# Attention: weighing in twelve half pieces, and turned tiles and projections one at a time

## The chip, the core and the metric

The kernel runs on one core of a Trainium2 chip. The metric is the device time of one execution in microseconds (us). TensorE (PE in the profile) multiplies and transposes into PSUM; ScalarE (ACT), VectorE (DVE) and GpSimd (POOL) work beside it, each through its own list of instructions in order, and they are tied together by semaphores. TensorE's clock is granted at one of two levels, 2.4 or 1.2 GHz; the profile gives it as 1.00 and 0.50.

## What is computed

Four layers on x of shape (4, 1024, 128): causal attention with 16 heads of 8 columns, a mixture of 8 experts, a sigmoid message layer, and the mixture again. The change touches the attention alone:

```python
k = _layernorm((x @ Wk).reshape(b, t, h, s), kln_w, kln_b)
q = _layernorm((x @ Wq).reshape(b, t, h, s), qln_w, qln_b)
v = (x @ Wv).reshape(b, t, h, s)
dot = jnp.einsum('bqhs,bkhs->bhqk', q, k) * scale
dot = jnp.where(causal, dot, -jnp.inf)
attn = jax.nn.softmax(dot, axis=-1)
out = jnp.einsum('bhqk,bkhs->bqhs', attn, v).reshape(b, t, e)
return out @ Wo + bo
```

## The kernel before

The attention works through 16 **groups**: 4 batches of 1024 tokens, and in each 4 groups of 4 heads. A head's queries and keys lie in 32 rows (the values in high and low parts, and the shift by the row's maximum), so that the four heads of a group fill the 128 rows of TensorE, and each product of queries and keys uses 32 rows of it and all 128 columns.

A group has 40 **steps**. In step i TensorE makes score product i of the group (`scores`, line 640; up to 512 columns) into one of six PSUM banks, and about one product for the maxima of the *next* group (`maxima_unit`, line 627). ScalarE takes the score bank away with an exponential (`weights`, line 822); VectorE takes the other away with a maximum (lines 1150 and 1155). The banks go round in a ring: unit n waits until unit n - 6 is taken.

Beside these products TensorE has **blocks** of another form. **Weighing** (`weigh`, line 660) multiplies the exponentials of key tile j by the values: 128 rows and 32 columns for each of the four heads, side by side, into the accumulator `o_acc` of two banks. The trace shows each of these float32 products as two records: `x16` there is 8 products. Tile j weighs for all queries at or after it: piece j has 1024 - 128 j columns, so pieces 0 to 3 run over both halves of the tokens. **Turns** (line 594) transpose four 128x128 tiles with all of TensorE: keys and queries of the group after next, the shifted queries (`turn_low`, `turn_high`), the results `oT`, and in the first group of a batch the tokens. **Projections** (line 612) are made for the next batch in groups with g == 1.

The function `sequence` writes the order of a group out by hand, and every engine reads the same order. Before the change it places the blocks so, by the step after which they come:

- weighing: pieces 0, 1, 2, 3, 4, 5 after steps 15, 20, 27, 32, 36, 39; pieces 6 and 7 of the group before together after step 5 (`WEIGHED_AFTER`, `WEIGHED_LATE`);
- `empty_out` at step 9: ScalarE copies all of `o_acc` to `oT`; both halves of `oT` are turned together after step 17, and VectorE divides them (`normalise`);
- keys and queries for later at 31, 32, 34 and 35; `turn_high` at 3, `turn_low` at 21;
- projections in pairs at 21, 23, 26 and 29, in groups with g == 1 only.

I call steps 0 to 14 of a group its **first stretch** and steps 15 to 39 its **second stretch**; they are told apart in the trace by the start of the exponentials.

## Time and profile before

| | us |
|---|---|
| median of three runs | 2903.04 |
| lowest and highest | 2891.97, 2903.37 |
| the profiled execution | 2907.53 |
| its span, first to last instruction | 2905.7 |
| attention: first to last exponential of its 16 groups | 65.9 to about 754 |
| PE, DVE, ACT busy in the whole span | 2671.1, 1784.2, 1597.3 |

The profile is of one execution. The rows below are of four groups of the attention, from 200.6 to 364.9 us: the fourth group of the first batch (200.6 to 237.2), the first of the second batch (to 275.0), the second (to 323.4) and the third (to 364.9). Their lengths are 36.6, 37.8, 48.4 and 41.5 us, and this pattern returns in the other batches. "Busy" counts overlapping products once, so it says nothing of how many run side by side. In the view in order of time, the first number is the start; the time that a block takes from its neighbours is best read from its start to the start of what comes after it.

### The profile page before, as it was taken

How to read it: one execution, taken by the hardware profiler on the slowest of the kernel's cores; microseconds unless marked ns; L12 is line 12 of the kernel's file. 1: busy time of each engine (PE TensorE's matmuls, PEld its weight loads, DVE VectorE, ACT ScalarE, POOL GpSimd, SP SyncE). 2: the span in 40 equal slices, each digit the busy share in tenths (PEclk: the TensorE clock that was granted, in tenths of full speed). 3: DMA queues.
4: the chain of work that ended last, by engine and by line, in shares of the span. 5: the costliest groups of instructions: out<-in, count | busy, mean ns of one | idle time of the engine just before them, and what ended most of it. 6: DMA issues, size and time to landing. Idle time of an engine off the chain costs nothing. (4 is left out here: it accounts for less than half of the span.)

```text
span 2905.7 us, 54730 instructions
## 1 busy us (share of the span) xinstructions
PE 2671.1 (92%) x18814; PEld 1641.2 (56%) x18814; DVE 1784.2 (61%) x4087; ACT 1597.3 (55%) x2918; POOL 811.9 (28%) x1179
## 2 busy tenths in 40 slices
PE   6988998999678979999999999999999999996897
PEld 4444443444367855666556555555555555554786
DVE  7677677667364755555665556555556655556556
ACT  2566666666554445555555556565566555554343
POOL 3142423423425321111111121112121133322542
PEclk7688877767899989999999999999999999997998
DMA  9000000000323438888888888877888788884222
GB/s 162 3 1 1 1 1 1 1 1 15 119 78 110 136 80 196 197 196 196 199 192 198 192 196 190 192 183 183 186 190 192 184 200 193 199 193 175 61 82 85
DMA packets 187362, 374.82 MB, mean 129 GB/s; under 512 B 44257, under 2 KB 99690, under 8 KB 185738
## 3 DMA queue, kind: packets, MB, share of 16 engines
q1 hardware_dynamic: 178506, 354.15, 51.1%
q0 software_dynamic: 8640, 17.84, 1.7%
q8 instruction: 129, 2.11, 0.3%
q14 instruction: 87, 0.71, 0.1%
HBM read 38.10 MB, written 39.86 MB: 27 GB/s over the span
## 5 line engine op out<-in xcount | busy, mean ns | idle before, releaser
L2996 DVE STREAM_TRANSPOSE m_turned<-m_sig 128x1024 f32<-128x1024 f32 x512 | 613.7, 1228 | 423.1 <-ACT m_sig L2766 222.6
L2589 PE MATMUL m_v_ps<-m_sig,m_tok 128*64 128x512 f32 x2048 | 468.1, 599 | 0.0
L2602 PE MATMUL m_v_ps<-m_sigT,m_tok 128*64 128x256 f32 x4064 | 461.2, 380 | 0.6 <-DMA m_sigT<-m_turned 0.6
L822 ACT ACTIVATE a_prob<-a_bank 128x512 f32<-128x512 f32 (+1 forms) x640 | 321.7, 564 | 222.0 <-PE a_bank L640 199.7
L2573 PE MATMUL m_f_ps<-m_swap,m_own 64*128 64x512 f32 x1536 | 426.0, 404 | 16.6 <-DMA m_swap<-m_own 8.4
L2573 PE MATMUL m_f_ps<-m_own,m_swap 64*128 64x512 f32 x1536 | 426.1, 404 | 0.0
L2602 PEld LDWEIGHTS m_v_ps<-m_sigT,m_tok 128*64 128x64 f32 x4064 | 289.9, 137 | 196.0 <-issue 59.2
L2766 ACT ACTIVATE m_sig<-m_f_ps 128x1024 f32<-128x1024 f32 x256 | 248.4, 1023 | 251.0 <-issue 152.6
L2862 POOL TENSOR_TENSOR m_own<-m_uv,m_own 128x1024 fp32r<-128x1024 f32 x64 | 151.9, 2373 | 810.5 <-ACT m_own L2728 810.5
L2573 PEld LDWEIGHTS m_f_ps<-m_swap,m_own 64*128 64x128 f32 x1536 | 271.7, 186 | 99.5 <-ACT m_sig L2752 25.9
L627 PE MATMUL a_bank<-a_kT,a_qT 32*128 32x512 f32 (+3 forms) x768 | 277.6, 496 | 31.8 <-DVE a_maxima L1155 20.2
L2752 ACT ACTIVATE m_sig<-m_f_ps 128x512 f32<-128x512 f32 x512 | 264.5, 604 | 38.7 <-PE m_f_ps L2573 37.0
L2589 PEld LDWEIGHTS m_v_ps<-m_sig,m_tok 128*64 128x64 f32 x2048 | 135.7, 136 | 265.2 <-issue 264.8
L2573 PEld LDWEIGHTS m_f_ps<-m_own,m_swap 64*128 64x128 f32 x1536 | 271.4, 186 | 5.6
L640 PE MATMUL a_bank<-a_qmT,a_kT 32*128 32x512 f32 (+3 forms) x768 | 247.0, 501 | 25.9 <-DVE a_maxima L1155 13.2
L1150 DVE TENSOR_REDUCE a_first_max<-a_bank 128x1 f32<-128x512 f32 x256 | 165.1, 684 | 91.8 <-PE a_bank L627 89.4
L640 PEld LDWEIGHTS a_bank<-a_qmT,a_kT 32*128 32x128 f32 x768 | 112.4, 220 | 167.5 <-issue 110.5
L2778 ACT CAST m_v1T_hi<-m_v_ps 128x256 fp32r<-128x256 f32 x128 | 47.8, 373 | 285.4 <-PE m_v_ps L2602 271.6
L660 PE MATMUL a_o_acc<-a_prob,v 128*32 128x512 f32 (+3 forms) x1536 | 198.1, 639 | 5.9 <-POOL a_prob L968 3.6
L627 PEld LDWEIGHTS a_bank<-a_kT,a_qT 32*128 32x128 f32 x768 | 138.1, 226 | 108.4 <-DVE a_maxima L1155 50.2
L3005 DVE TENSOR_TENSOR m_v1T_lo<-m_v_ps,m_v1T_hi 128x256 fp32r<-128x256 f32 x128 | 54.2, 423 | 217.0 <-ACT m_v1T_hi L2778 205.6
L1773 PE MATMUL f_y_ps<-f_w_down,f_innerT 128*128 x1136 | 153.3, 278 | 25.8 <-DVE f_raw L2183 17.9
(505 smaller groups left out, 4426.5 us busy)
## 6 DMA issues: line engine op xcount, KB each, us to landing
m_sigT<-m_turned SPq DMA_DIRECT2D x2042, 128.0 KB, 2.3
m_swap<-m_own SPq DMA_DIRECT2D x64, 256.0 KB
f_t_rows<-f_sent_rows SPq DMA_DIRECT2D x142, 65.0 KB
f_sent_rows<-a_proj SPq DMA_DIRECT2D x34, 260.0 KB, 8.9
m_swap<-m_own SPq DMA_DIRECT2D x64, 128.0 KB
f_h<-back_rows SPq DMA_DIRECT2D x8, 512.0 KB, 5.0
rows<-back_rows SPq DMA_DIRECT2D x6, 512.0 KB, 4.2
x<-in_L_attn_a_x_dram SPq DMA_DIRECT2D x4, 512.0 KB, 4.8
```

Source lines behind the costliest of these rows:

```text
L627: mm = pe.matmul(out[:, col:col + k1 - k0], qT[G % 2][rows, qt * P:(qt + 1) * P], kT[G % KEPT_KEYS][rows, k0:k1], start=True, stop=True)
L640: mm = pe.matmul(out[:, col:col + q1 - q0], kT[G % KEPT_KEYS][rows, j * P:(j + 1) * P], qmT[G % 2][rows, q0:q1], start=True, stop=True)
L660: mm = pe.matmul(o_acc[h * STACK:(h + 1) * STACK, q0:q1], v1[:, j, g * GROUP + h, :], weights_at[:, h, q0 - off:q1 - off], start=(j == 0), ...
L822: act.activation(to[:, h, start:start + width], src[:, 0:width], ACT.Exp).then_inc(u.free(), 1)
L1150: ins = dve.tensor_reduce(first, scores, AX.X, ALU.max)
L1773: mm = pe.matmul(y_ps[:, 0:DIM], innerT[p][:, ib * P:(ib + 1) * P], w_down[:, ds(e * INTER + ib * DIM, DIM)], start=(ib == 0), stop=(ib == ...
L2573: mm = pe.matmul(f_ps[s][:, cols], tile_of(u[rows, :], j + s * SIDE), v[rows, cols], start=start, stop=stop)
L2589: mm = pe.matmul(v2_ps[h * RANK:(h + 1) * RANK, :], tok[p][:, 0, j + s * SIDE, :], sig[j % 2][s][:, h * HALF:(h + 1) * HALF], start=(j == ...
L2602: mm = pe.matmul(v1_ps[h * RANK:(h + 1) * RANK, g * 2 * P:(g + 1) * 2 * P], tok[p][:, 1, jj, :], sigT[g][:, :, 2 * h:2 * h + 2, jj, :].rea ...
L2752: ins = act.activation(sig[1][s][:, cols], f_ps[s][:, cols], ACT.Sigmoid)
L2766: act.activation(sig[j % 2][s][:, :], f_ps[s][:, :], ACT.Sigmoid).then_inc(sig_ready, 1)
L2996: dve.transpose(turned[g][:, :, q, :, :], sig[j % 2][s][:, :].rearrange("p (t j a) -> p j t a", j=4, a=STACK)).then_inc(turn_ready, 1)
```

## The change

Each piece of weighing for tiles 0 to 3 is cut into a part for the low half of the queries (columns 0 to 511) and one for the high half, so that there are twelve pieces (tile, half) of at most 512 columns. They are placed anew. `o_acc` is emptied in two halves with a semaphore each. The turns of `oT`, keys, queries and tokens, and each projection, get a step of their own. Number and size of the products stay as they are. `late_made` and `state` only hand the numbers of the score units over from group to group.

```diff
-        WEIGHED_AFTER = {15: (0,), 20: (1,), 27: (2,), 32: (3,), 36: (4,), 39: (5,)}
-        WEIGHED_LATE = (6, 7)
+        WEIGHED_AFTER = {9: (0, 0), 12: (1, 0), 14: (0, 1), 18: (1, 1), 24: (2, 0), 26: (3, 0), 28: (2, 1), 31: (3, 1), 36: (4, 1)}
+        WEIGHED_LATE = {1: (5, 1), 4: (6, 1), 5: (7, 1)}
...
+        PROJECTED_AT = (17, 19, 21, 23, 25, 27, 30, 32)
...
-                if prev and i == 3:
+                if prev and i == 2:
                     yield "turn_high", 0
-                if prev and i == 5:
-                    for n in WEIGHED_LATE:
-                        yield "weigh", n
-                if prev and i == 9:
+                if prev and i in WEIGHED_LATE:
+                    yield "weigh", WEIGHED_LATE[i]
+                if prev and i == 7:
+                    yield "empty_out", 1
+                if i == 29:
                     yield "empty_out", 0
-                if two_ahead and i in (31, 32, 34, 35):
-                    yield ("keys", "queries")[i // 34], (31, 32, 34, 35).index(i) % HALVES_OF
+                if two_ahead and i in (16, 30, 34, 38):
+                    yield ("keys", "queries")[i in (30, 38)], (16, 30, 34, 38).index(i) // 2
...
-                if prev and i == 17:
-                    for n in range(HALVES_OF):
-                        yield "turn_out", n
-                if prev and g == 0 and i in (23, 29):
-                    for n in range(HALVES_OF):
-                        yield ("turn_tokens", "project_out")[i == 29], n
+                if prev and i == 11:
+                    yield "turn_out", 1
+                if i == 33:
+                    yield "turn_out", 0
+                if prev and g == 0 and i in (17, 19, 23, 25):
+                    yield ("turn_tokens", "project_out")[i // 23], (17, 19, 23, 25).index(i) % HALVES_OF
...
-                    if i in (21, 23, 26, 29):
-                        for n in range(2):
-                            yield "project", 2 * (21, 23, 26, 29).index(i) + n
+                    if i in PROJECTED_AT:
+                        yield "project", PROJECTED_AT.index(i)
...
+                q0, q1 = max(j * P, half * HALF), (half + 1) * HALF
+                weights_at, off = prob_of(j, q0)
+                last = j == (half + 1) * HALF_T - 1
+                for h in range(GROUP):
+                    mm = pe.matmul(o_acc[h * STACK:(h + 1) * STACK, q0:q1], v1[:, j, g * GROUP + h, :],
+                                   weights_at[:, h, q0 - off:q1 - off], start=(j == 0), stop=last)
+                if last:
+                    mm.then_inc(weighed[half], 1)
...
-                act.wait_ge(weighed, G + 1)
-                act.copy(oT[:, :], o_acc[:, :]).then_inc(o_free, 1)
+                act.wait_ge(weighed[half], G + 1)
+                act.copy(half_of(oT, half), half_of(o_acc, half)).then_inc(o_free[half], 1)
```

Two places of TensorE's list show it, both in the fourth group (qmT1 and kT0 are its shifted queries and keys; kT1 and qT0 belong to the next group, whose maxima are made; `a_o_acc` is a piece of weighing). The first is around steps 11 to 15, before:

```order
L640 MATMUL a_bank4<-a_qmT1,a_kT0 128x512
L627 MATMUL a_bank5<-a_kT1,a_qT0 128x512
L640 MATMUL a_bank0<-a_qmT1,a_kT0 128x512
L627 MATMUL a_bank1<-a_kT1,a_qT0 128x512
L640 MATMUL a_bank2<-a_qmT1,a_kT0 128x512
L627 MATMUL a_bank3<-a_kT1,a_qT0 128x512
L640 MATMUL a_bank4<-a_qmT1,a_kT0 128x512
L627 MATMUL a_bank5<-a_kT1,a_qT0 128x512
L660 MATMUL a_o_acc<-a_prob0,v1 32x512 x8
```

And now, steps 9 to 12:

```order
L628 MATMUL a_bank0<-a_kT1,a_qT0 128x512
L660 MATMUL a_o_acc<-a_prob0,v1 32x512 x4
L641 MATMUL a_bank1<-a_qmT1,a_kT0 128x512
L628 MATMUL a_bank2<-a_kT1,a_qT0 128x512
L641 MATMUL a_bank3<-a_qmT1,a_kT0 128x512
L628 MATMUL a_bank4<-a_kT1,a_qT0 128x512
L595 MATMUL a_bank5<-ident,a_oT 128x128 x4
L641 MATMUL a_bank0<-a_qmT1,a_kT0 128x512
L628 MATMUL a_bank1<-a_kT1,a_qT0 128x512
L660 MATMUL a_o_acc<-a_prob1,v1 32x384 x4
```

Piece 0, eight products in one go after ten steps of 32-row products alone, has become two pieces of four, and the first of them, a turn of `oT` and the low piece of tile 1 now stand within steps 9 to 12.

The second place is around steps 32 to 35 of the same group, before:

```order
L660 MATMUL a_o_acc<-a_prob0,v1 32x128 x4
L660 MATMUL a_o_acc<-a_prob1,v1 32x512 x4
L640 MATMUL a_bank4<-a_qmT1,a_kT0 128x384
L627 MATMUL a_bank5<-a_kT1,a_qT0 128x512
L640 MATMUL a_bank0<-a_qmT1,a_kT0 128x384
L594 MATMUL a_bank1<-ident,q_st 128x128 x4
L627 MATMUL a_bank2<-a_kT1,a_qT0 128x512
L640 MATMUL a_bank3<-a_qmT1,a_kT0 128x384
L594 MATMUL a_bank4<-ident,q_st 128x128 x4
L627 MATMUL a_bank5<-a_kT1,a_qT0 128x512
```

And now, from step 31 on:

```order
L660 MATMUL a_o_acc<-a_prob1,v1 32x512 x4
L641 MATMUL a_bank2<-a_qmT1,a_kT0 128x384
L628 MATMUL a_bank3<-a_kT1,a_qT0 128x512
L641 MATMUL a_bank4<-a_qmT1,a_kT0 128x384
L628 MATMUL a_bank5<-a_kT1,a_qT0 128x512
L595 MATMUL a_bank0<-ident,a_oT 128x128 x4
L641 MATMUL a_bank1<-a_qmT1,a_kT0 128x384
L595 MATMUL a_bank2<-ident,k_st 128x128 x4
L628 MATMUL a_bank3<-a_kT1,a_qT0 128x512
```

The low part of tile 3 has gone from in front of its high part to step 26, and a turn of the low half of `oT`, that of the group itself, has come in at step 33.

## Rows read from the trace of the kernel before

**Rows 1.** Busy time by stretch, two stretches to a group; PEclk is the granted clock.
```profile
core 0: us, PE busy (x) PEld busy (x) DVE busy (x) ACT busy (x) POOL busy (x), PEclk, DMA share, GB/s
200.60:210.70 10.10, 9.37 (x51) 4.65 (x48) 8.79 (x37) 8.76 (x18) 5.85 (x15) 0.65 0.01 2
210.70:237.20 26.50, 26.24 (x177) 11.89 (x176) 17.73 (x52) 14.49 (x30) 3.21 (x9) 0.87 0.00 1
237.20:247.30 10.10, 7.97 (x56) 3.64 (x58) 9.34 (x39) 9.43 (x18) 5.90 (x15) 0.87 0.01 2
247.30:275.00 27.70, 27.64 (x201) 14.17 (x199) 20.85 (x61) 15.66 (x33) 3.20 (x9) 0.92 0.00 1
275.00:293.50 18.50, 11.95 (x60) 5.82 (x64) 15.79 (x64) 12.77 (x22) 5.85 (x15) 0.60 0.01 2
293.50:323.40 29.90, 29.83 (x196) 14.09 (x189) 17.38 (x51) 19.13 (x49) 3.23 (x10) 0.96 0.00 1
323.40:339.00 15.60, 10.07 (x52) 4.85 (x48) 14.29 (x41) 11.74 (x21) 10.23 (x12) 0.60 0.01 2
339.00:364.90 25.90, 25.46 (x177) 11.90 (x176) 17.76 (x53) 14.55 (x31) 15.98 (x22) 0.91 0.00 1
```

**Rows 2.** Who waited for whom, 200.6 to 237.2: in total, times, longest.
```profile
ACT a_prob L822 <- PE a_bank L640: 12.8, 8, 3.6
```

**Rows 3.** TensorE in order of time, clock high: start, length, line, operation.
```profile
214.35 0.38 PE L640 MATMUL a_bank<-a_qmT,a_kT 32*128 32x256 f32 x1
...
215.01 1.09 PE L594 MATMUL a_bank<-ident,a_oT 128*128 128x128 f32 x8
...
217.87 1.71 PE L660 MATMUL a_o_acc<-a_prob,v 128*32 128x384 f32 x16
...
219.51 0.49 PE L640 MATMUL a_bank<-a_qmT,a_kT 32*128 32x512 f32 x1
...
220.16 0.66 PE L594 MATMUL a_bank<-ident,q_st 128*128 128x128 f32 x4
220.75 0.50 PE L640 MATMUL a_bank<-a_qmT,a_kT 32*128 32x512 f32 x2
...
234.25 1.06 PE L660 MATMUL a_o_acc<-a_prob,v 128*32 128x512 f32 x8
...
235.24 0.46 PE L640 MATMUL a_bank<-a_qmT,a_kT 32*128 32x256 f32 x6
...
235.90 0.85 PE L660 MATMUL a_o_acc<-a_prob,v 128*32 128x384 f32 x8
...
236.68 0.49 PE L640 MATMUL a_bank<-a_qmT,a_kT 32*128 32x512 f32 x1
```

**Rows 4.** The same view where the clock is at half.
```profile
525.03 1.12 PE L594 MATMUL a_bank<-ident,k_st 128*128 128x128 f32 x4
526.07 0.79 PE L627 MATMUL a_bank<-a_kT,a_qT 32*128 32x512 f32 x1
...
534.71 0.79 PE L627 MATMUL a_bank<-a_kT,a_qT 32*128 32x512 f32 x1
...
535.86 1.94 PE L660 MATMUL a_o_acc<-a_prob,v 128*32 128x512 f32 x8
537.72 0.59 PE L640 MATMUL a_bank<-a_qmT,a_kT 32*128 32x256 f32 x3
```

**Rows 5.** Busy time by stretch as in rows 1, cut where the clock changed.
```profile
327.30:339.40 12.10, 7.09 (x22) 3.21 (x21) 11.33 (x22) 8.74 (x14) 6.73 (x7) 0.50 0.01 2
339.40:343.00 3.60, 3.60 (x17) 0.60 (x16) 1.05 (x2) 0.17 (x1) 3.38 (x4) 0.50 0.00 0
343.70:360.60 16.90, 16.46 (x116) 8.53 (x115) 12.98 (x39) 10.99 (x23) 10.54 (x14) 1.00 0.00 1
521.30:541.00 19.70, 19.45 (x90) 8.12 (x83) 7.72 (x21) 8.21 (x16) 5.39 (x13) 0.50 0.00 1
613.40:655.40 42.00, 40.21 (x175) 20.88 (x177) 27.24 (x92) 23.78 (x47) 12.26 (x23) 0.50 0.00 1
```

More of the change, by code:

```diff
@@ L416, in attention_phase @@
         queries_rounded, queries_ready = sem("a_queries_rounded"), sem("a_queries_ready")
-        unit_full, kept, weighed, o_free = (sem(n) for n in ("a_unit_full", "a_kept", "a_weighed", "a_o_free"))
+        unit_full, kept, weighed, o_free = sem("a_unit_full"), sem("a_kept"), *([sem(f"a_{n}_{half}") for half in ("low", "high")] for n in ("weighed", "o_free"))
         unit_free = [sem(f"a_unit_free{i}") for i in range(RINGS)]
@@ L700, in count, with group @@
                 pe.matmul(out[:, 2 * ROUTE:2 * ROUTE + P], k["ones"][:, :], k["below"][:, :], start=True, stop=True).then_inc(unit_full, 1)
-            def group(u, b, g, prev, prep, follows, shifted, stacks, high=None):
+            def group(u, b, g, prev, prep, follows, shifted, stacks, late_made, normed, high=None):
                 G = GROUPS * b + g
-                ahead, last_of_prev = (g + 1) % GROUPS, u.n
-                score_made, next_stacks, z_made, normed, turned, shifted_high = {}, [], [], [], [], high
+                ahead, normed = (g + 1) % GROUPS, dict(normed)
+                score_made, next_stacks, z_made, turned, shifted_high = {}, [], [], [], high
                 for what, n in sequence(g, prev, prep, follows, stage_of(b, g)):
@@ L709, in group @@
                         scores(u, G, n, {0: (shifted,), FIRST_HIGH: (shifted_high,)}.get(n, ()))
-                        for piece in SCORES[n][0]:
-                            score_made[piece[0]] = u.n
+                        for j, q0, _ in SCORES[n][0]:
+                            score_made[j, q0 // HALF] = u.n
                     elif what == "keys":
@@ L746, in group, with before_batch @@
                         count(u)
-                return shifted, next_stacks
+                return shifted, next_stacks, {piece: score_made[piece] for piece in WEIGHED_LATE.values()}, {0: normed[0]}
+            def before_batch(shifted, stacks, late_made, normed):
+                return (shifted - UNITS_BATCH, [n - UNITS_BATCH for n in stacks], {piece: n - UNITS_BATCH for piece, n in late_made.items()},
+                        {0: normed[0] - UNITS_BATCH})
             u = Units(0, 0)
@@ L761, in _ @@
             high = turn_shifted(u, 0, 0, 1)
-            shifted, stacks = group(u, 0, 0, False, False, True, shifted, (), high)
+            state = group(u, 0, 0, False, False, True, shifted, (), {}, {}, high)
             for b in range(BATCH - 1):
@@ L771, in _ @@
             for g in (1, 2, 3):
-                shifted, stacks = group(u, b, g, True, False, g < GROUPS - 1, shifted, stacks)
-            for n in WEIGHED_LATE:
-                weigh(u, b, GROUPS - 1, n, u.n)
-            normed = [turn_out(u, GROUPS * BATCH - 1, n) for n in range(HALVES_OF)]
+                state = group(u, b, g, True, False, g < GROUPS - 1, *state)
+            _, _, late_made, normed = state
+            for piece in WEIGHED_LATE.values():
+                weigh(u, b, GROUPS - 1, *piece, late_made[piece])
+            normed[1] = turn_out(u, GROUPS * BATCH - 1, 1)
             turned = [turn_tokens(u, n, normed[n]) for n in range(HALVES_OF)]
@@ L858, in group @@
                     elif what == "empty_out":
[L859 to L860 removed]
+                        empty_out(G - n, n)
+                        if g == 0 and n and prev:
                             values(u, projects)
@@ L1428, in _ @@
                 made = group(u, link, b, g, True, False, g < GROUPS - 1, masked_by, made)
-            for n in range(HALVES_OF):
-                normalise(u, link, GROUPS - 1, n)
+            normalise(u, link, GROUPS - 1, 1)
             u.n += HALVES_OF
```

53 lines of the change are left out of this document (20 added, 33 removed).

## The prediction

> **What bounds the kernel now.** I read the busy time by stretch first. In the second stretch of each group TensorE is busy almost without a break: 26.24 of 26.5 us in the fourth group, 27.64 of 27.7, 29.83 of 29.9 and 25.46 of 25.9 in the three after it, while VectorE has 17.4 to 20.9 and ScalarE 14.5 to 19.1 [rows 1]. In the first stretch it is otherwise: VectorE has 8.79 of 10.1, 9.34 of 10.1, 15.79 of 18.5, 14.29 of 15.6, and TensorE has room, most of it in the last two (11.95 of 18.5, 10.07 of 15.6) [rows 1]. Then the waits: over the fourth group ScalarE's exponentials waited 12.8 us for score products [rows 2]. So TensorE sets the pace for steps 15 to 39, and VectorE (with ScalarE close by) for steps 0 to 14. No engine sets it for the whole group, and the time is more than the sum of any of them: 36.6 us, against 26.5 of VectorE and 23.3 of ScalarE.
>
> The third view is the granted clock. It is 0.60 to 0.87 in the first stretches and 0.87 to 0.96 in the second ones [rows 1]. Cut at its changes, it shows a cycle: it is at half (1.2 GHz) while TensorE has ten steps of 32-row products and waits (327.3 to 339.4, busy 7.09 of 12.1 us), still at half during piece 0, sixteen records in one go in which TensorE is busy all 3.60 us, and at full (2.4 GHz) after it [rows 5]. Where the drop in the first stretch costs little, since VectorE bounds it, piece 0 at half clock costs its doubling.
>
> **The change part by part.** Prices are from start to start, clock full [rows 3]: pieces 1 together (384 and 512 columns) 219.51 - 217.87 = 1.64 us; a lone 512-column piece 235.24 - 234.25 = 0.99; a lone 384-column piece 236.68 - 235.90 = 0.78; a turn of four tiles 220.75 - 220.16 = 0.59; one step of products alone between two blocks 220.16 - 219.51 = 0.65; two steps between two blocks 215.01 - 214.35 = 0.66. The last two say that products of different heads run side by side, so an interruption after every second step costs TensorE little and one after every step doubles the steps.
>
> *Cutting.* A piece cut in two costs 0.99 + 0.78 - 1.64 = 0.13 us more. The fourth group goes from 14 blocks to 20, so about 0.8 us are added per group.
>
> *Moving.* Out of the second stretch go pieces (0,0), (0,1), (1,0) and (5,1): 2 x 0.99 + 2 x 0.78 = 3.5 us, and half the turn of oT, 0.6. They come into the first stretch, where TensorE had to wait for VectorE.
>
> *TensorE's sum for a fourth group, all at full clock.* Six 512-column pieces 5.9; two of 384, 1.6; for two of 256 and two of 128 no row stands alone, and the slope between 512 and 384 (0.21) gives 0.57 and 0.36, together 1.9. Eight turns 4.7. The 40 steps lie in 20 runs, about 0.66 each, 13.2; four of these have three or four steps, and I add 0.5 for each. The sum is 29.3 us. VectorE's is 8.79 + 17.73 = 26.5, and where it set the pace it was busy 9.34 of 10.1 us, 92% [rows 1], so 28.8. The bounds are nearly equal and are joined by a ring of six banks, so neither is hidden fully: I take **31 us**, against 36.6, a gain of 5.6. If they overlapped perfectly it would be 29.3; if they hid nothing more than now, the group loses only the doubling of piece 0, (3.60 of rows 5 less 2 x 0.99) = 1.6, less 0.8 for cuts. Both ends stay for the range. I take 31 since moving 3.5 us changes the balance directly.
>
> *First group of a batch.* VectorE has 9.34 + 20.85 = 30.2, over 0.92 = 32.8; two turns of tokens and two projections of the output are added to TensorE's sum. I take 35 against 37.8: a gain of 3.
>
> *Second group.* Its first stretch, 18.5 us, is set by VectorE (the token moments) and stays. The second loses 3.5 + 0.6, but eight projections stand alone in place of four pairs: four more joints at 0.13 and some five runs cut from two steps to one. I take a gain of 1.5 in 48.4.
>
> *Third group.* The first stretch (15.6) is VectorE's. With the clock full the second would be about 20 in place of 25.9.
>
> *ScalarE and GpSimd.* The copy of oT was one instruction; two halves add a fraction of one microsecond per group to an engine with 23.3 busy of 36.6. The high half is asked for at step 7, two steps after piece (7,1) rather than four; TensorE runs up to three steps ahead in the ring, so I cost that wait at nothing; at worst it is one piece, 0.4. The masks of tiles 0 and 1 come after steps 3 and 7, and their pieces wait at 9 and 12: five or more steps, some 3 us. The tail of the last group changes by under 1 us.
>
> **The clock** is the term with two signs. For a high clock: the ten steps of 32-row products before piece 0 become four at most (6 to 9), and six steps in the second stretch become three. Against it: after the change nothing like piece 0 is left; the longest piece is eight records. The trace shows half clock that did not end although TensorE was busy 19.45 of 19.7 us (521.3 to 541.0) and 40.21 of 42.0 (613.4 to 655.4) [rows 5]; these hold all other pieces and turns, and what ended them was the next piece 0. At half clock a turn costs 526.07 - 525.03 = 1.04, a 512-column piece 537.72 - 535.86 = 1.86, two steps 535.86 - 534.71 = 1.15 [rows 4]. A whole group of the new order at half: pieces 6 x 1.86 + 2 x 1.45 + 3.2 = 17.3, turns 8.3, 20 runs x 1.1 = 22: 47.5 us against 36.6. VectorE's long steps in the second and third groups (token moments, sums of squares) will still let the clock drop there. The projections of a second group and of a first group's output lie densely, so I expect the clock to come back there; in a third group I give it one chance in two, and two in three that the fourth group runs at full.
>
> The Trainium skill ("TensorE: Matmul & The Clock Gate", section "Why this matters for your kernels") advises to keep TensorE continuously busy to have the full clock. By that rule the evener order would always be at full, which is the second rival below; the two half-clock stretches of rows 5, busy 95% and more, speak against it being enough.
>
> **The sum.** Per batch: second group -1.5; third 0 (-5.5 or +5, even); fourth 2/3 x -5.6 + 1/3 x +8 = -1; the next first group 7/8 x -3 + 1/8 x +8 = -1.6; together -4. Three batches, -12. The old order's own long half-clock stretches, 19.7 and 42.0 us [rows 5], are part of the time before: at prices near double on about half of the work they cost some 8 and 12 us, and the chances above already stand for their like after. That is -20. The opening group and the last three give -3. Together -35, from the profiled execution's 2907.5 to 2872.5; the median shown is 4.5 lower, and I predict **2870 us** (-1.1%).
>
> **The rivals.**
> - *Wash* (2889 to 2917, centre 2903): TensorE is no longer alone the bound, and VectorE's and ScalarE's turns in the ring take what it gives back; only piece 0's doubling goes, and the cuts eat it. For it: VectorE already at 85 to 92% in the first stretches. Against: ScalarE's 12.8 us of waiting for scores.
> - *Always full clock*: no drop in the third and fourth groups and the first. Per batch -5.5 - 5.6 - 3 - 3 = -17, three times, with the 20 above: -71, so 2832.
> - *Slower, by the clock*: once at half in a second or third group, nothing lifts it before the next projections. Third +5, fourth +11, first +7, second -1: +22 per batch, +66 in three, less the 20: +46, so 2949. It decides when more than about half of the fourth groups run at half.
>
> **How the numbers follow.** Forecast (2845 to 2888) 0.50, wash 0.20, always full 0.10, slower by the clock 0.20. A measurement of this kernel can tell about 0.5% (14.5 us) from no change. Faster by more than that: 0.50 + 0.10 = 0.60, within it 0.20, slower 0.20. The range takes forecast, always full and wash, and a little of the slow side: 2825 to 2920.
>
> **What would show it.** Forecast: fourth groups of 30 to 33 us; TensorE and VectorE both at 85% or more in each stretch; ScalarE's wait for scores in one group down from 12.8 to under 8; mean clock of the attention at least 0.80. The slow rival: granted clock 0.50 across whole third and fourth groups, groups over 44 us, TensorE busy throughout. The wash: groups of 35 to 37 at full clock with TensorE waiting for VectorE. I am wrong on the runs if two steps between blocks take 1.2 us in place of 0.66 at full clock. Outside the attention nothing should move by more than a microsecond or two.

## The result, and the profile after

| | before | changed |
|---|---|---|
| median of four runs | 2903.05 | 2992.2 |
| lowest and highest | 2891.97, 2903.37 | 2975.54, 3000.57 |
| the profiled execution | 2907.53 | 2999.59 |

The changed kernel takes 1.031 times as long, with a 95% interval of 1.0253 to 1.0366. I had forecast 2870 us and a range up to 2920: the forecast is wrong in sign, and the time lies outside the range. My slower rival had the right mechanism, but put it at 2949 us, 43 below the measured time.

From the page of the changed kernel: its span, the busy time of the engines, and the granted clock in 40 slices of the span (tenths of full speed).

```profile
span 2997.8 us, 54746 instructions
...
PE 2820.3 (94%) x18814; PEld 1686.7 (56%) x18814; DVE 1794.6 (60%) x4087; ACT 1618.3 (54%) x2934; POOL 810.6 (27%) x1179
...
PEclk6565555657568998999999999999999999998998
```

TensorE executes as many records as before (18814), but is busy for 2820.3 us in place of 2671.1. Over the attention (up to 890 us, the first 12 slices) the clock is mostly at 5 and 6 tenths. VectorE is up by 10.4 us and ScalarE by 21.0. The loss is one of speed, not of waiting.

Busy time by stretch in the changed kernel, with the columns of [rows 1]: the fourth group of the first batch, and the first, second and third of the second batch; then a long piece of them; then the whole attention and what follows it.

```profile
core 0: us, PE busy (x) PEld busy (x) DVE busy (x) ACT busy (x) POOL busy (x), PEclk, DMA share, GB/s
214.20:232.90 18.70, 18.47 (x95) 6.85 (x93) 10.48 (x40) 8.93 (x18) 5.96 (x15) 0.52 0.00 1
232.90:260.60 27.70, 27.63 (x135) 12.48 (x135) 16.48 (x48) 15.70 (x32) 3.06 (x8) 0.61 0.00 1
260.60:280.50 19.90, 19.09 (x95) 7.17 (x93) 10.52 (x41) 9.93 (x20) 5.96 (x15) 0.50 0.00 1
280.50:318.80 38.30, 38.26 (x159) 20.05 (x158) 21.04 (x59) 17.28 (x34) 3.06 (x8) 0.50 0.00 1
318.80:343.00 24.20, 21.48 (x97) 8.27 (x97) 16.26 (x64) 12.41 (x22) 5.98 (x15) 0.50 0.01 1
343.00:391.70 48.70, 48.66 (x156) 21.34 (x157) 17.27 (x48) 21.33 (x49) 3.06 (x8) 0.50 0.00 0
391.70:413.50 21.80, 19.26 (x94) 6.99 (x93) 15.80 (x44) 12.04 (x22) 13.77 (x14) 0.50 0.00 1
413.50:444.50 31.00, 29.64 (x134) 13.69 (x135) 16.53 (x48) 15.83 (x31) 12.42 (x18) 0.50 0.00 1
239.00:464.30 225.30, 217.53 (x909) 94.22 (x908) 119.25 (x372) 108.87 (x211) 51.77 (x96) 0.50 0.00 1
66.50:890.10 823.60, 784.57 (x3680) 346.42 (x3682) 484.36 (x1560) 448.70 (x882) 229.67 (x411) 0.58 0.02 5
890.10:2997.80 2107.70, 1992.03 (x15018) 1312.89 (x15010) 1260.47 (x2381) 1154.45 (x2014) 553.81 (x726) 0.98 0.70 171
```

The four groups last 46.4, 58.2, 72.9 and 52.8 us, where [rows 1] give 36.6, 37.8, 48.4 and 41.5. The granted clock is 0.50 in six of the eight stretches, and it stays there without a break from 239.0 to 464.3, for 225 us, although TensorE is busy for 217.5 of them. In [rows 5] the longest such stretch was 42.0 us. Over the whole attention the clock is 0.58.

The wait that I watched, over the fourth group, which answers [rows 2]:

```profile
ACT a_prob L825 <- PE a_bank L641: 17.9, 14, 2.3
```

ScalarE waits 17.9 us for score products in place of 12.8; I had looked for under 8. TensorE bounds the first stretch now, too: it is busy for 18.47 of 18.70 us there, and VectorE for only 10.48.

Before any of this is read as the change's doing, the profile of before needs a second look. Here are the attention and what follows it in the first profile of before, then in a second execution of the same kernel (b0_before_again, below).

```profile
65.90:753.50 687.60, 623.00 (x3676) 297.93 (x3675) 476.55 (x1558) 430.36 (x866) 230.48 (x411) 0.76 0.03 6
753.50:2905.70 2152.20, 2005.75 (x15022) 1316.79 (x15022) 1257.87 (x2383) 1151.75 (x2014) 554.30 (x726) 0.98 0.68 167
```

```profile
65.30:786.80 721.50, 650.37 (x3680) 308.28 (x3678) 480.31 (x1558) 431.84 (x865) 230.24 (x411) 0.73 0.03 6
786.80:2901.90 2115.10, 1996.67 (x15022) 1313.28 (x15014) 1259.61 (x2383) 1155.73 (x2014) 554.34 (x726) 0.98 0.69 170
```

The same program took 34 us less in the attention and 37 us more after it in the execution that I had worked from, and the two totals are 2907.5 and 2903.7. In the profiles of the experiments what follows the attention took 2109.5 to 2115.3 us on three chips, whatever the order, and 2149.5 to 2159.8 on a fourth, so that this part may go by the chip; which chip the profiles of before and of the changed kernel come from, the records don't say. So against b0 the attention lost 102 us (823.6 less 721.5) and the rest gave back 7.

### The profile page after: what moved, and what is told of

The parts are those of the page before. It is cut to its first block and busy times, and to the rows that moved or that the text cites. A ratio compares the mean times of both kernels' runs of the same rounds, so it can differ in the third digit from the quotient of the medians.

```text
span 2997.8 us, 54746 instructions
## 1 busy us (share of the span) xinstructions
PE 2820.3 (94%) x18814; PEld 1686.7 (56%) x18814; DVE 1794.6 (60%) x4087; ACT 1618.3 (54%) x2934; POOL 810.6 (27%) x1179
## 5 line engine op out<-in xcount | busy, mean ns | idle before, releaser
L825 ACT ACTIVATE a_prob<-a_bank 128x512 f32<-128x512 f32 (+1 forms) x640 | 333.4, 557 | 317.4 <-PE a_bank L641 253.6
L628 PE MATMUL a_bank<-a_kT,a_qT 32*128 32x512 f32 (+3 forms) x768 | 306.1, 573 | 26.3 <-DVE a_maxima L1158 20.7
L641 PE MATMUL a_bank<-a_qmT,a_kT 32*128 32x512 f32 (+3 forms) x768 | 286.7, 599 | 4.7 <-ACT a_prob L825 3.4
L660 PE MATMUL a_o_acc<-a_prob,v 128*32 128x512 f32 (+3 forms) x1536 | 265.9, 782 | 6.4 <-POOL a_prob L971 3.6
L641 PEld LDWEIGHTS a_bank<-a_qmT,a_kT 32*128 32x128 f32 x768 | 130.7, 266 | 233.9 <-issue 219.6
L628 PEld LDWEIGHTS a_bank<-a_kT,a_qT 32*128 32x128 f32 x768 | 155.6, 279 | 100.7 <-issue 52.1
L1158 DVE CUSTOM_DVE_ANT_0 a_masked_out<-a_bank,mask,a_first_max 128x128 f32<-128x128 f32 (+3 forms) x256 | 129.0, 548 | 86.1 <-PE a_bank L628 78.0
L968 POOL TENSOR_TENSOR a_steps<-ones 128x1 f32<-128x1 f32 x128 | 24.9, 194 | 567.0 <-ACT a_prob L825 566.9
```

What stands on the lines that cost most here:

```text
L628: mm = pe.matmul(out[:, col:col + k1 - k0], qT[G % 2][rows, qt * P:(qt + 1) * P], kT[G % KEPT_KEYS][rows, k0:k1], start=True, stop=True)
L641: mm = pe.matmul(out[:, col:col + q1 - q0], kT[G % KEPT_KEYS][rows, j * P:(j + 1) * P], qmT[G % 2][rows, q0:q1], start=True, stop=True)
L660: mm = pe.matmul(o_acc[h * STACK:(h + 1) * STACK, q0:q1], v1[:, j, g * GROUP + h, :], weights_at[:, h, q0 - off:q1 - off], start=(j == 0), ...
L825: act.activation(to[:, h, start:start + width], src[:, 0:width], ACT.Exp).then_inc(u.free(), 1)
```

## The experiments

Each run is compared with runs of the kernel before on the same chip. I give its median, the ratio with its 95% interval, and from its profile the length of the attention and the share of it at half clock, for some also the run's mean clock. For comparison: b0 has 721.5 us, 54% at half and 0.908; the changed kernel 823.6 us, 84% at half and 0.862. The chips differ, so that losses and gains against the changed kernel are best taken from the ratios. Where I say at which step the clock rises, it is the step whose exponential had last begun; each such count is from one profile, over the 15 groups after the first.

**The same kernels again.** No edit. b0_before_again is the kernel before, f1_changed_again the changed one.

> The kernel before, unchanged, profiled once more. In the first profile its attention took 688 us and what follows it 2152; in the changed kernel and the first four experiments what follows took 2108 to 2114. If the 40 us belong to that one execution and not to the kernel, what follows the attention takes 2105 to 2120 here, and the attention 690 to 735. If they belong to the kernel before, it is 2150 again.

2903.72 us in a single run. The attention took 721.5 us and what follows it 2115.1, as expected if the 40 us belonged to the one execution.

> The changed kernel, unchanged, once more on the chip of c2 and c3. Attention 810 to 830 with clock 0.5 through whole groups, as in its first profile, if that state is the kernel's own and not one execution's; what follows the attention 2105 to 2160 by the chip.

2969.83 us in a single run; attention 789.3 us, 75% at half, clock 0.877. The attention is 21 us below the range that I expected, and 34 us shorter than in the first profile of the same kernel. Two groups that hold the same work, both the fourth of their batch, in this one execution, and then the whole attention:

```profile
197.50:231.80 34.30, 33.67 (x227) 14.92 (x228) 27.51 (x88) 23.93 (x49) 9.04 (x23) 0.90 0.00 1
399.30:445.60 46.30, 46.02 (x227) 19.34 (x227) 27.02 (x88) 24.55 (x49) 9.03 (x23) 0.57 0.00 1
65.00:854.30 789.30, 746.15 (x3684) 327.19 (x3682) 483.85 (x1560) 446.28 (x882) 230.55 (x411) 0.62 0.02 4
```

Both have 227 records, and TensorE is busy for 98% and 99% of both. One is at 0.90 and takes 34.3 us, the other at 0.57 and takes 46.3. This is the cleanest view of the case: the order can be faster than 36.6 us, and the clock decides whether it is. The second groups of this execution show it as well: 50.7 us with 34% at half, 72.9 with all of it at half.

**Piece 0 in one go again, all else as changed.** The two halves of tile 0 stand together after step 14 and (1,0) after 16:

```diff
-        WEIGHED_AFTER = {9: (0, 0), 12: (1, 0), 14: (0, 1), 18: (1, 1), ...
+        WEIGHED_AFTER = {14: ((0, 0), (0, 1)), 16: ((1, 0),), 18: ((1, 1),), ...
```

> The changed kernel with one thing undone: the two halves of piece 0 stand together again after step 14 (sixteen records in one go), piece (1,0) goes to step 16; all else as changed. Theory 1 (clock: the new order has no unbroken run long enough to bring the clock back to full, so it stays at half through whole groups): the mean granted clock of the attention comes back from 0.58 to about 0.76, and the time from 2992 to 2900 or below. Theory 2 (interruptions: twenty blocks in a group in place of fourteen cost time at either clock): one block fewer in twenty, so within 10 us of 2992.

2906.82 us, 1.0036 [1.0010, 1.0063]; attention 728.7 us, 58% at half, clock 0.904. A fourth group in its two stretches, and the attention:

```profile
201.70:218.60 16.90, 16.67 (x87) 7.50 (x88) 10.26 (x40) 8.78 (x19) 6.02 (x15) 0.53 0.01 1
218.60:245.70 27.10, 26.78 (x142) 12.05 (x143) 16.47 (x48) 15.74 (x31) 3.08 (x8) 0.67 0.00 1
66.00:794.70 728.70, 676.19 (x3684) 307.87 (x3682) 482.30 (x1560) 441.61 (x882) 231.24 (x411) 0.71 0.03 6
```

Moving two pieces, (0,0) from step 9 to 14 and (1,0) from 12 to 16, takes back 0.027 of the 0.031. The clock shows it directly: it rises at steps 14 to 16 in 14 of the 15 groups, and in 4 of them in the changed kernel (6 in f1). The work is the same to the record (3684 against 3680 seen), and TensorE's busy time falls from 784.6 to 676.2. But nothing of the hoped gain appears: the group is 44.0 us, and its first stretch is 16.9 against 10.7 in b0.

**One step between the halves of piece 0.** As the last, with:

```diff
-14: ((0, 0), (0, 1)),
+13: ((0, 0),), 14: ((0, 1),),
```

> The kernel of a1 (the changed kernel with both halves of piece 0 after step 14; it took 2907) with one thing different: the low half comes after step 13 and the high half after step 14, so that one step of 32-row products stands between them. Number, size and neighbourhood of the pieces stay. Theory 1 (the clock comes back only with a long unbroken run of products that use the whole array): mostly lost, clock of the whole run from 0.904 to 0.87 or 0.88, 2945 to 2985. If it is only the place that matters (weighing late in the first stretch, little of it before), it stays within 10 us of 2907.

2976.75 us, 1.0119 [1.0075, 1.0163]; attention 756.3 us, 64% at half. By its ratio it lies between the two expectations. A single step between two runs of eight records costs 0.8% against a1's ratio, so an unbroken run counts for something; the clock rises at steps 13 to 16 in 9 of the 15 groups, where a1 has 14. But the other 1.9% of a1's gain is there with the run broken: it comes with (0,0) and (1,0) moved next to (0,1), and no run separates their nearness from their later place.

**More work in the changed order.** `turn_tiles` writes its four tiles several times over into the same bank, so that only work is added. a2 does it five times for the high half of `oT` alone (after step 11):

```diff
-                for i, t in enumerate(tiles):
-                    mm = pe.transpose(out[:, i * P:(i + 1) * P], src(t), k["ident"][:, :])
+                for _ in range(times):
+                    for i, t in enumerate(tiles):
+                        mm = pe.transpose(out[:, i * P:(i + 1) * P], src(t), k["ident"][:, :])
```

> The changed kernel with work added: the turn of the high half of oT at step 11 is made five times over into the same bank instead of once (16 transposes more in each of 15 groups, at full clock 16 x 0.11 = 1.75 us, in all 26 us; at half clock twice that). Theory 1 (clock): the added run lifts the clock in most groups, attention clock over 0.8, and the time falls although work was added: 2992 - 71 - 89 + 26 = about 2858 if my sum at full clock was right, 2900 if only half of the groups are lifted. Theory 2 (interruptions): only the added work shows, 2992 + 26 to 52, so 3018 to 3044.

2921.97 us, 1.0104 [1.0070, 1.0137]; attention 747.2 us, 54% at half. Work was added and, by the ratios, two thirds of the loss went away (0.021 of 0.031). The clock rises at step 11 or 12, at the fivefold turn, in all 15 groups, and in one of them in the changed kernel. It does not stay up, though: the attention's mean clock is 0.73, where I expected over 0.8. c1 does it five times for both halves of `oT` and both turns of the queries, four turns to a group.

> The changed kernel with four turns of each group (both of oT, both of the shifted queries) made five times over: 64 transposes more a group, 7.0 us at full clock. It is to hold the clock at full and so to measure the new order there. If my sum of TensorE at full clock (29.3 us for a fourth group) was right, a fourth group takes 36 to 38 us and the attention about 690 at a clock over 0.9. If the many blocks cost more than I summed, fourth groups take over 42 us although the clock is full.

2903.36 us in a single run; attention 725.0 us, 21% at half, clock 0.951. The fourth group comes out as expected, and the attention is 35 us longer than I expected. A fourth group, the attention, and TensorE in order of time around one of the turns:

```profile
205.30:241.80 36.50, 35.99 (x292) 20.51 (x293) 27.43 (x88) 23.69 (x50) 9.03 (x23) 1.00 0.00 1
67.10:792.10 725.00, 677.48 (x4650) 382.51 (x4654) 480.75 (x1559) 434.58 (x882) 231.09 (x411) 0.89 0.03 6
```

```profile
224.19 2.40 PE L596 MATMUL a_bank<-ident,q_st 128*128 128x128 f32 x20
226.51 0.51 PE L642 MATMUL a_bank<-a_qmT,a_kT 32*128 32x512 f32 x3
```

A fivefold turn takes 226.51 - 224.19 = 2.32 us, a single one 0.59 [rows 3], so each repetition costs 0.43 and the sixteen in a group 6.9. The group is at full clock throughout and takes 36.5 us; less the 6.9 that is 29.6, beside the 29.3 of my sum for TensorE at full clock.

c2 adds the same to the *kernel before*, to see what the order is worth when the clock is mostly high in both.

> The kernel before with the same added work as in c1: both turns of oT and both of the shifted queries five times over, 7.0 us a group at full clock. It measures the old order at full clock, to set beside c1 (fourth group 36.5 us, attention 725). My sum of TensorE for the old order at full clock was 32.6 for a fourth group, so 38 to 40 with the added work and an attention of 755 to 775: the new order is then the better one by 2 to 3 us a group where the clock is full. If the order made no difference at full clock, 36.5 and 725.

2931.53 us in a single run; attention 748.1 us, 28% at half.

```profile
208.10:249.20 41.10, 39.81 (x295) 22.34 (x290) 26.71 (x89) 23.11 (x47) 9.10 (x24) 0.92 0.00 1
66.80:814.90 748.10, 688.02 (x4634) 388.75 (x4634) 479.55 (x1557) 426.53 (x865) 230.03 (x411) 0.86 0.01 4
```

The new order is 4.6 us better with the same added work in a fourth group (36.5 against 41.1) and 23 us over the attention. Part of that is still clock, since the fourth group has 1.00 against 0.92. These are one run each, on two chips, but what follows the attention is alike, within 6 us. Then the smaller doses, in the changed order. c3: three times for all four turns. c4: twice. c5: three times for `oT` alone.

> The changed kernel with the same four turns made three times over instead of five: 3.5 us a group at full clock, 56 in all, half of c1's. If the clock is held as in c1 (0.95 over the run), the attention falls from 725 to about 670 and the kernel to 2850. If the shorter runs (1.3 us at full clock, 2.6 at half) no longer bring the clock back, it stays low in the third and following groups as in the changed kernel: 2960 to 3010.

2879.39 us, 0.9930 [0.9901, 0.9958]; attention 696.5 us, 27% at half, clock 0.943.

```profile
199.20:232.20 33.00, 32.50 (x261) 17.24 (x260) 27.27 (x88) 23.66 (x50) 9.04 (x23) 1.00 0.00 1
67.90:764.40 696.50, 639.16 (x4172) 332.23 (x4170) 482.50 (x1560) 436.12 (x881) 230.85 (x411) 0.87 0.01 4
```

It beats both kernels: 0.7% under the one before, and by the ratios 3.7% under the changed one (on this chip the single run of f1 is 3.1% above it), though it does some 56 us of useless transposes (16 groups of 3.5). Its fourth group takes 33.0 us, or 29.5 without the 3.5.

> The changed kernel with the same four turns made twice: 16 transposes more a group, 1.75 us at full clock, 28 in all. If the clock is held as in c3, attention about 668 and the kernel 2850. If runs of 0.9 us at full clock and 1.7 at half are too short, whole groups at half come back as in the changed kernel, 2930 to 2980. c3 had already one second stretch at half (steps 16 to 33 of a third group), so I lean to something between, 2890 to 2930.

2922.15 us (2896.82 to 2958.2), 1.0146 [1.0050, 1.0242]; attention 742.5 us, 54% at half.

> The changed kernel with only the two turns of oT (steps 11 and 33) made three times over, the shifted queries once: 1.75 us a group at full clock, as in c4, but in two runs of the length of c3's. In c3 the clock rose at 11 or 12 and at 33, and at 21. If it is the length of a run that counts, this holds the clock better than c4, 2865 to 2900; if it is the amount of work, the same as c4.

2927.31 us (2912.78 to 2937.99), 1.0225 [1.0160, 1.0289]; attention 734.8 us, 47% at half. Both add half of what c3 adds, c4 in shorter runs and c5 at fewer places, and both stay slower than the kernel before. By the ratios, c4 has taken back 0.016 and c5 0.009 of the 0.038 between the changed kernel and c3. Their intervals overlap, and so the times don't tell whether the length of one run or the amount in a group counts. The kernel before stood at 2875.59 us (2855.21 to 2904.69) in these runs, lower than in the others on the same chip (2899.32); against that 2899.32 the two would stand at 1.008 and 1.010, within their spread of each other.

The traces say something about the length. Take the groups in which the clock is at half when step 11 begins, and count those in which it rises at step 11 or 12, where the high half of `oT` is turned. Turned once (the changed kernel, f1) it is 1 of 15 and 1 of 14; twice (c4) 5 of 13; three times (c5, c3) 11 of 13 and 10 of 11; five times (a2, c1) 15 of 15 and 12 of 12. So the longer the run of transposes at this place, the oftener the clock rises there. How long it then stays up is another matter, as a2 and c5 show with 54% and 47% at half.

**The parts of the change apart.** a3 leaves the weighing where it was before the change (both halves of a tile behind each other, at 15, 20, 27, 32, then (4,1) at 36, (5,1) at 39, the last two tiles at 5), empties the high half at 8 and the low at 35, turns the low half at 37, and keeps the rest of the change: turns and projections alone.

> One part of the change: turns and projections alone and oT emptied and turned in halves as in the changed kernel (the low half later, emptied at step 35 and turned at 37), but the pieces of weighing together and at their old steps 15, 20, 27, 32, 36, 39 and 5. Theory 1 (clock): piece 0 is there in one go, so the clock comes back as before: 2903 give or take 15. Theory 2 (interruptions): the turns and projections account for two of the six added blocks a group and the eight lone projections: about a third to a half of the loss, 2930 to 2950.

2894.41 us, 0.9999 [0.9966, 1.0031]; attention 714.5 us, 52% at half. a4 is the other part: the weighing as changed, and keys, queries, tokens, output and projections in pairs at the old places.

> The other part: the twelve pieces of weighing at their new steps and oT in halves, but keys, queries, tokens, output projections and input projections at their old steps, in their old pairs (31, 32, 34, 35; 23 and 29; 21, 23, 26, 29). Theory 1 (clock): no piece 0 in one go, so the clock stays low in third and fourth groups; the pairs of projections may lift it in second ones: 2960 to 2990. Theory 2 (interruptions): four blocks more than before, 2930 to 2960.

2954.98 us (2942.55 to 2980.57), 1.0197 [1.0131, 1.0263]; attention 800.6 us, 78% at half. Taken as a time, this is where I put theory 2 (2930 to 2960); the 78% at half speaks for the clock, and so do a1, with one block fewer than the changed kernel, and a2, with more work, which both took far less time than theory 2 gave them. So turns and projections alone cost nothing while piece 0 is whole, and the cut and moved weighing costs 2.0%. The whole change costs 3.1%. With piece 0 gone, the pairs of projections still lift the clock in a4: it rises at step 21, the first pair, in all three second groups that have projections. TensorE in order of time just before one of these rises, at 145.3:

```profile
141.07 2.93 PE L615 MATMUL a_bank<-w_qkv,a_zT 128*128 128x384 f32 x4
143.79 1.06 PE L597 MATMUL a_bank<-ident,q_st 128*128 128x128 f32 x4
```

The change takes those pairs apart too. That this is the whole of the remaining 1.1% is not shown.

**Work out of the first stretch.** d2 is a1 with the first stretch as light as before the change: (0,0) and (0,1) at 15, (1,0) at 17, (1,1) at 18, (5,1) at 39, the late pieces together at 5, the shifted queries at 3, the high half emptied at 8 and turned at 15. d1 spreads more evenly what comes behind a whole piece 0: 15 whole, then single pieces at 18, 20, 23, 25, 27, 29, 33 and 37, with the turns of `oT` at 15 and 32.

> The kernel of a1 with the first stretch as light as in the kernel before: piece (5,1) back at step 39, (6,1) and (7,1) together at step 5, the shifted queries at 3, the high half of oT turned right behind piece 0, which stands at step 15; the second stretch stays as in the changed kernel. If blocks in the first stretch are not hidden (TensorE stands blocked in order by VectorE's long instructions, and the blocks come behind), the first stretches go from 17, 22 and 21 us (fourth, second, third groups) back to 10 to 11, 18.5 and 15.6, and the second ones grow by 1 to 3: 2907 - 16 x 3 = about 2860. If my claim was right that the first stretch hides what stands there, it gets slower: 2920.

2962.39 us, 1.0058 [1.0042, 1.0074]; attention 738.3 us, 56% at half.

```profile
205.20:215.90 10.70, 9.95 (x55) 5.02 (x49) 8.65 (x37) 8.58 (x17) 4.50 (x11) 0.50 0.01 2
215.90:244.90 29.00, 28.72 (x179) 12.28 (x177) 18.01 (x52) 15.60 (x31) 3.57 (x10) 0.79 0.00 1
```

> A version meant to beat both: first stretch as in the kernel before; piece 0 whole at step 15, the high half of oT and the first turn of keys right behind it (5.4 us in one go at half clock); then no more than three steps between blocks: (1,0) 18, (1,1) 20, (2,0) 23, (2,1) 25, (3,0) 27, (3,1) 29, (4,1) 33, (5,1) 37, turns and projections alone as in the changed kernel. Theory 1: the clock is lifted at 15 in every group and held longer; clock of the whole run 0.92 or more, 2845 to 2870. If half clock returns in steps 20 to 27 all the same, 2870 to 2895.

2953.61 us, 1.0020 [0.9995, 1.0044]; attention 729.7 us, 56% at half. Both missed what I expected by their ratios. d2's first stretch is back at 10.7 us from the 16.9 of a1, and its second stretch is 29.0 against 27.1, so this group is 4.3 us shorter; the attention as a whole is not, 738.3 against 728.7. In a1, d2 and d1 the share at half clock is 56 to 58%, and their ratios lie within 0.4% of each other, wherever the blocks stand.

**A longer run in the kernel before.** b1 moves the turn of `oT` behind piece 0, one line; b2 moves piece 1 there as well.

```diff
-                if prev and i == 17:
+                if prev and i == 15:
```

> The kernel before with one thing moved: both halves of oT are turned right behind piece 0, after step 15, and not after 17. No work is added; the unbroken run with all 128 rows grows from 3.4 to 5.4 us at half clock. Theory 1 (the clock comes back only with a long unbroken run): fewer groups in which it is missed; attention clock from 0.76 to 0.80 or more, 2870 to 2890. Theory 2 (the clock has nothing to do with the order; what counts is the number of blocks): one block fewer of fourteen, 2899 give or take 10.

2888.28 us, 0.9956 [0.9925, 0.9988]; attention 719.1 us, 54% at half.

> The kernel before with piece 0, the two turns of oT and piece 1 all together after step 15: about 4.4 us in one go at full clock and 8.4 at half. Theory 1: the clock is brought back in every group, also after a drop in the stretch before it; 2860 to 2885. Theory 2, and the view that splitting is good because it keeps ScalarE and VectorE supplied: the long block starves both for 4 us in each group, 16 x 2 or more, 2930 and above.

2901.46 us, 1.0010 [0.9980, 1.0040]; attention 716.1 us, 55% at half. b1's time is within what theory 1 gave, its attention clock of 0.73 is not; b2 fits neither theory. In both the clock comes up at step 15 in all 15 groups, where b0 has it at 15 to 17 in 9 and the first profile of before in 14; in b0's other six it comes at step 20, where piece 1 stands, which is also sixteen records in one go. And then it drops again: at step 20 in five groups of b1 and not at all before the next group in five others, at 20 to 25 in every group of b2, where almost only 32-row products stand between step 15 and step 27. A longer run at one place bought nothing measurable in b2 and 0.4% in b1; the share at half clock did not move. c1 and c3 have their repetitions at four places, and there it did.

## Why the prediction was wrong, point by point

**"So TensorE sets the pace for steps 15 to 39": right, and its sum was right.** At full clock I had 29.3 us for TensorE in a fourth group. c1 gives 29.6 without the added work and c3 29.5. Whether the two bounds cost each other something (my 31) these two can't tell, since the added work keeps TensorE well ahead of VectorE. f1 has the nearest case without it: 34.3 us at a mean clock of 0.90, that is with about 6.9 us at half clock; if that part took half as long at full clock, an estimate, the group would take 31. The single prices held as well: in the changed kernel at full clock a piece of 256 columns took 166.97 - 166.40 = 0.57 us and one of 128 took 167.69 - 167.33 = 0.36, the values that I had taken from a slope. TensorE in order of time:

```profile
166.40 0.64 PE L660 MATMUL a_o_acc<-a_prob,v 128*32 128x256 f32 x8
166.97 0.44 PE L628 MATMUL a_bank<-a_kT,a_qT 32*128 32x384 f32 x1
...
167.33 0.43 PE L660 MATMUL a_o_acc<-a_prob,v 128*32 128x128 f32 x8
167.69 0.43 PE L628 MATMUL a_bank<-a_kT,a_qT 32*128 32x384 f32 x1
```

**"So I expect the clock to come back there" and "two in three that the fourth group runs at full": this is the step that failed.** Third groups are at half clock for 79 to 100% of their time in this profile and the fourth ones for 48 to 85%; not one of either is at full. The second stretch of the second group of the second batch has eight projections in its 48.7 us, and the clock is 0.50 in all of them. The change sets each of them apart from the next; TensorE in order of time there:

```profile
351.67 1.65 PE L613 MATMUL a_bank<-w_qkv,a_zT 128*128 128x384 f32 x2
353.25 0.80 PE L641 MATMUL a_bank<-a_qmT,a_kT 32*128 32x512 f32 x2
353.84 0.63 PE L628 MATMUL a_bank<-a_kT,a_qT 32*128 32x128 f32 x4
354.40 1.65 PE L613 MATMUL a_bank<-w_qkv,a_zT 128*128 128x384 f32 x2
355.84 1.06 PE L595 MATMUL a_bank<-ident,q_st 128*128 128x128 f32 x4
```

A projection of 1.58 us, 1.15 us of two steps of 32-row products, a projection, a turn, two steps: TensorE never waits, and the clock does not come back. It is not so in each second group with projections: in the first and third batch the clock is back by step 15 and 18, and their second stretches last 27.8 and 30.7 us. In f1 it is back in the first batch alone. The same groups in f1 differ by 22 us with the clock (50.7 and 72.9). I had the evidence in my hands. I wrote of rows 5 that "what ended them was the next piece 0", and that "after the change nothing like piece 0 is left"; then I gave the clock good chances all the same, because projections "lie densely", which says only that TensorE is busy. a1 bears that sentence out: with piece 0 whole again, 0.027 of the 0.031 is gone. e2 limits it: most of that is there with the two halves one step apart, so that "like piece 0" means weighing close together as much as one unbroken run.

The Trainium skill ("TensorE: Matmul & The Clock Gate", section "Why this matters for your kernels") advises to keep TensorE busy without a break to have the full clock. I had set it against rows 5 and given it 0.10. The 225.3 us at 0.50 with TensorE busy for 217.5 of them say it more clearly: for this mix of 32-row products and short blocks, busy is not sufficient. In c3 TensorE is busy for less of the attention than in the changed kernel (92% against 95%), and the clock is 0.87 there against 0.58.

**"Once at half in a second or third group, nothing lifts it before the next projections": right in kind, a size off.** The signs given for it are all there. Its terms against the measured ones: the fourth group +11, measured 46.4 - 36.6 = 9.8; the third +5, measured +11.3; the first group +7, measured +20.4; the second -1, measured +24.5. All but the fourth group's are too low, and the last two the most. I priced the first group with VectorE's bound in mind, and the second as if its projections brought the clock back; both ran wholly at half. At half clock the first group's second stretch takes 38.3 us against 27.7 [rows 1], TensorE busy for 38.26. The four terms come to +66 for these four groups where I had +22. The fourth group's +11 was my own price of a whole group at half (47.5 us), while the forecast's sum took +8 for it. No other four groups in a row lose as much: the other second groups last 52.0, 55.0 and 52.7 us, and over the whole attention the loss is 136 us against the first profile of before, 102 against b0.

**"The old order's own long half-clock stretches" as 20 us to win back: wrong in size, since one profile was read as the kernel.** In b0 the old order's attention is 34 us longer, and what follows it 37 us shorter. The fourth groups of its first two batches last 36.6 us there as well, but its first and third groups are longer than in [rows 1], 41.8 and 53.4 us against 37.8 and 41.5:

```profile
247.60:289.40 41.80, 40.23 (x252) 19.99 (x249) 30.50 (x99) 25.18 (x51) 9.14 (x25) 0.76 0.00 1
...
338.50:391.90 53.40, 46.60 (x227) 21.12 (x224) 32.36 (x92) 26.97 (x51) 27.17 (x35) 0.60 0.00 1
```

A third group of the old order can thus be as long as one of the new (52.8). And the pattern of the four lengths, which I said returns in the other batches, does so only loosely in the first profile itself: the third batch's third group takes 49.9 us there and the fourth batch's first 56.6. Rows 5 had shown me one draw, and the "-20" in my sum and in both clock rivals hangs on it; no change of the clock's course between two executions was in the working.

**"They come into the first stretch, where TensorE had to wait for VectorE": half wrong.** The first stretches grew from 18.5 to 24.2 us (second group) and from 15.6 to 21.8 (third), and from 10.1 to 18.7 and 19.9 in the fourth and first. Half clock is part of that, but c1 still has 23.2 to 23.7 and 20.4 to 21.7 in the second and third groups of its first three batches, at half for 33 to 47% of them and with about 3.5 us of added turns in each; c3, with half of these, has 22.6 to 23.2 and 18.6 to 18.9. Here is what the waits show. Busy time and TensorE's waits in a third group's first stretch, in b0 and then in the changed kernel (163.7 to 183.1):

```profile
157.60:173.20 15.60, 9.05 (x55) 4.45 (x50) 14.29 (x42) 11.73 (x20) 10.23 (x12) 0.74 0.00 1
```

```profile
PEld a_bank L627 <- DVE a_maxima L1155: 4.6, 3, 3.5
PE a_bank L627 <- DVE a_maxima L1155: 3.6, 2, 3.2
```

```profile
163.70:183.10 19.40, 16.09 (x94) 5.88 (x94) 15.87 (x44) 11.81 (x21) 13.68 (x14) 0.68 0.01 2
```

```profile
PEld a_bank L628 <- DVE a_maxima L1158: 4.1, 3, 3.4
PE a_bank L628 <- DVE a_maxima L1158: 3.3, 2, 3.1
```

About half of TensorE's free time there in b0, and nearly all of it in the changed kernel, is one wait of over 3 us for a bank that VectorE holds, at a product for the maxima; its length is nearly the same, 3.5 and 3.4 us. A block that stands behind the waiting product in TensorE's list starts after it; one that stands ahead of it is hidden only as far as TensorE would have stood waiting at that earlier place. This last is argued from the order of the list; no run tests it by itself. So the free 5.5 us of [rows 1] were real, but only a part of them could be used: TensorE's busy time in this stretch grows by 7.0 us (9.05 to 16.09, part of it by the lower clock), its free time shrinks by 3.2 (6.55 to 3.31), and the stretch grows by the other 3.8. What stays free is that one wait. d2 adds that it works the other way as well: taking the blocks out again shortens the first stretch and lengthens the second.

**ScalarE's copy of `oT` in two halves, priced at a fraction of one microsecond a group: not contradicted.** a3 has the two half copies and the turns alone and stands at 0.9999.

**The chances.** I gave the slower clock 0.20. Since the two long half-clock stretches of rows 5 ended at a piece 0 and at nothing else, and the change leaves no such piece, it should have been the forecast.

What stays open: what exactly lifts the clock and what keeps it up. Piece 0 whole (a1), piece 1 in b0, fivefold turns at one place (a2) and threefold turns at four places (c3) lift it, to different degrees; one step between the halves of piece 0 takes part of it away (e2); c4 and c5 show that a longer run lifts it oftener, and don't say whether length or amount holds it. The runs also leave open whether an order of useful work alone can reach c3's 27% at half.

## What to carry to other kernels

When an order of short blocks is changed, price it once at each of the two clock levels and then ask of each long half-clock stretch what ended it; if the change removes that, the low price is the forecast, however busy TensorE is. Spreading whole-array blocks evenly between products that use a part of the array can hold the clock down, and here a run kept together was worth more than the stalls that it makes (a1 against the changed kernel). An idle share is room for more work only as far as the idle time is not one wait that stands at another place of the same list, and one execution of a kernel whose clock oscillates is a sample, not its profile.

## What the runs showed of the hardware that I had not expected

- Half clock held for 225.3 us while TensorE was busy for 96.6% of it (217.53 us), and the same 227 records took 34.3 us at 0.90 and 46.3 at 0.57 within one execution.
- Useless work made the kernel faster: 3.5 us of repeated transposes in a group of the changed order took the ratio to the kernel before from 1.031 to 0.993 (2992.2 and 2879.39 us). Plain float32 transposes with all 128 rows are enough to bring the clock to 1.00 over a whole group, 36.5 and 33.0 us long.
- The part behind the attention, which the change doesn't touch, took 2109.5 to 2115.3 us on three chips and 2149.5 to 2159.8 on another.
- How often the clock rises at a turn goes with the length of the turn: in 1 of 15 groups for four transposes in one go, 5 of 13 for eight, 11 of 13 for twelve, 15 of 15 for twenty.
